# A graph attention kernel: two row sums of head 2 moved around head 1's scores, head 1's W2 casts behind a new wait, two roundings of head 2 moved ahead of its sums

## What is computed

```python
def gat_layer(x, W, a_s, a_d, b, edge_index, concat):
    n = x.shape[0]
    H, C = a_s.shape
    h = (x @ W).reshape(n, H, C)
    src, dst = (edge_index[0], edge_index[1])
    alpha_s = jnp.einsum('nhc,hc->nh', h, a_s)
    alpha_d = jnp.einsum('nhc,hc->nh', h, a_d)
    e = jax.nn.leaky_relu(alpha_s[src] + alpha_d[dst], NEG_SLOPE)
    m = jax.ops.segment_max(e, dst, num_segments=n)
    e = jnp.exp(e - m[dst])
    denom = jax.ops.segment_sum(e, dst, num_segments=n)
    alpha = e / (denom[dst] + EPS)
    msg = h[src] * alpha[:, :, None]
    out = jax.ops.segment_sum(msg, dst, num_segments=n)
    ...
h = gat_layer(x, W1, a_src1, a_dst1, b1, edge_list, concat=True)
h = jax.nn.elu(h)
out = gat_layer(h, W2, a_src2, a_dst2, b2, edge_list, concat=True)
...
x = _layernorm(x + out)
```

## Time and profile before

| | us |
|---|---|
| median of 3 executions | 650.02 |
| lowest, highest | 649.62, 650.75 |
| the profiled execution, its own time | 650.08 |
| its span in the profile | 648.3 |
| PE busy in it | 634.2 |
| DVE busy | 514.4 |
| ACT busy | 333.9 |
| POOL busy | 207.3 |

### The profile page before, as it was taken

How to read it: one execution, slowest core, us unless ns; L and a number is a source line. 1 busy time by engine, 2 the same in 40 slices (tenths; PEclk the granted TensorE clock), 3 DMA queues, 4 the chain that set the end, 5 groups by cost and what they waited for, 6 DMA issues and landing times.

```text
span 648.3 us, 9280 instructions
## 1 busy us (share of the span) xinstructions
PE 634.2 (98%) x3418; PEld 542.3 (84%) x3418; DVE 514.4 (79%) x929; ACT 333.9 (52%) x562; POOL 207.3 (32%) x121
## 2 busy tenths in 40 slices
PE   6999999999989999999999999999999999999996
PEld 4766668989868878988899889988998899887885
DVE  8999997798997977466855776566898588899676
ACT  6799991545614644353444544363445444534282
POOL 0000000131653550257224731465126614551230
PEclk9999999999999999999999999999999999999999
DMA  8422420115142620133203240216025401800002
GB/s 304 169 62 86 143 102 25 49 50 195 37 159 90 203 73 1 50 98 124 73 28 95 79 140 26 68 55 191 5 85 184 122 25 50 288 28 1 1 2 98
DMA packets 22173, 59.36 MB, mean 92 GB/s; under 512 B 2544, under 2 KB 2800, under 8 KB 22128
## 3 DMA queue, kind: packets, MB, share of 16 engines
q1 hardware_dynamic: 22128, 58.76, 27.9%
HBM read 54.03 MB, written 4.72 MB: 91 GB/s over the span
## 4 chain that ended last, share of the span: by engine, by line
PE 86%; DVE 11%; issue 2%; ACT 1%; DMA 0%; SPq 0%; DVEq 0%; ACTq 0%
PE O L1193 23%; PE R L1088 10%; PE R L1094 10%; PE R L1091 10%; PE O L1105 9%; PE R L1160 5%; PE R L1166 5%; PE R L1163 5%; PE R L1110 1%; DVE hl L711 1%; DVE junk L814 1%; DVE junk L686 1%; DVE rb L772 1%; PE O L1160 1%; PE O L1163 1%
## 5 line engine op out<-in xcount | busy, mean ns | idle before, releaser
L1022 POOL TENSOR_TENSOR W2l<-Wr,W2h 128x768 fp32r<-128x768 f32 x48 | 95.3, 1996 | 212.7 <-ACT W2h L405 212.7
L1026 POOL TENSOR_TENSOR Pl<-L,Ph 128x512 fp32r<-128x512 f32 x34 | 54.0, 1598 | 169.2 <-ACT Ph L454 169.2
L1088 PE MATMUL R<-W1h,xTh 128*128 128x384 f32 x312 | 105.8, 339 | 0.0
L1094 PE MATMUL R<-W1h,xTl 128*128 128x384 f32 x312 | 104.8, 336 | 0.0
L1091 PE MATMUL R<-W1l,xTh 128*128 128x384 f32 x312 | 104.8, 336 | 0.0
L686 DVE CUSTOM_DVE_ANT_0 junk<-h,abc 128x768 bf16<-128x768 f32 x64 | 64.4, 1007 | 41.1 <-ACT h L417 36.8
L1193 PE MATMUL O<-W2h,gh 128*128 128x256 f32 (+1 forms) x384 | 78.1, 338 | 0.0
L1193 PE MATMUL O<-W2h,gl 128*128 128x256 f32 (+1 forms) x384 | 77.1, 336 | 0.0
L1193 PE MATMUL O<-W2l,gh 128*128 128x256 f32 (+1 forms) x384 | 77.0, 335 | 0.0
L417 ACT COPY h<-R 128x384 f32<-128x384 f32 x62 | 29.5, 477 | 80.9 <-PE R L1094 72.4
L1160 PE MATMUL R<-Ph,hh 128*128 128x512 f32 x168 | 66.8, 398 | 2.6 <-DVE rb L772 1.7
(11 more groups left out here) (178 smaller groups left out, 1175.4 us busy)
## 6 DMA issues: line engine op xcount, KB each, us to landing
Wr<-in_W SPq DMA_DIRECT2D x101, 384.0 KB, 3.3
abc<-in_as SPq DMA_DIRECT2D x9, 384.0 KB, 4.4
abc<-in_ad SPq DMA_DIRECT2D x9, 384.0 KB, 6.0
h_rows<-h SPq DMA_DIRECT2D x8, 384.0 KB, 2.3
hl<-h_rows SPq DMA_DIRECT2D x8, 384.0 KB, 5.6
xin<-in_xT SPq DMA_DIRECT2D x6, 256.0 KB, 6.5
xr<-in_x SPq DMA_DIRECT2D x1, 1536.0 KB, 7.7
out<-res SPq DMA_DIRECT2D x4, 384.0 KB, 2.3
```

What stands on the lines that cost most here:

```text
L1022: e.tensor_tensor(W2l[:, m % N2, :], Wr[:, n, :], W2h[:, m % N2, :].bitcast(f32), ALU.subtract).then_inc(s_w2l, 1)
L1026: e.tensor_tensor(Pl[:, t, d0:d1], L[:, t, d0:d1], Ph[:, t, d0:d1].bitcast(f32), ALU.subtract).then_inc(s_Pl, 1)
L1088: e.matmul(bank[:, 0:HALF], xTh[:, f, xs], hi[:, ws], start=f == 0, stop=False)
L1094: m = e.matmul(bank[:, 0:HALF], xTl[:, f, xs], hi[:, ws], start=False, stop=f == FT - 1)
```

## The change

Four edits, all in heads 1 and 2, and all in the order of work or in what it waits for; nothing is computed in another way.

```diff
@@ scalar_program, head 1
                     high_w2(0, 4)
                     high_w2(0, 5)
+
+                    e.wait_ge(s_hl, 2 * NT)
                     for k in range(3):
                         high_w2(1, k)
@@ scalar_program, head 2
                     scores(2, 2, 0, NT, ring_bank("r2", 2, 0), ...)
+                    high_h(2, 0)
+                    high_h(2, 1)
                     high_sums(2)
-                    for t in range(NT):
-                        high_h(2, t)
+                    high_h(2, 2)
+                    high_h(2, 3)
                     for k in range(3, FT):
                         high_w1(3, k)
@@ vector_program
-            def sums_P(h):
+            def sums_P(h, between=None):
 
                 e.wait_ge(s_sd, 3 * h + 2)
                 e.scalar_tensor_tensor(
                     out=y2[:, :], in0=y2[:, :], scalar=EPS / 128, in1=rb[:, :], op0=ALU.add, op1=ALU.add).then_inc(s_sd, 1)
+                if between:
+                    between()
                 e.wait_ge(s_dh, h)
@@
                 if h == 1:
-                    scores(1, 1, 0, NT, ring_bank("r1", 1, 0), 6)
-                    sums_P(1)
-                    for t in (2, 3):
+                    def sums_2(t):
                         e.wait_ge(s_h32, 16 + 2 * t + 2)
                         sums_h(2, t, h32[:, t % 2, :], abc[:, 0, :, :])
+                    sums_2(2)
+                    scores(1, 1, 0, NT, ring_bank("r1", 1, 0), 6)
+                    sums_P(1, lambda: sums_2(3))
                     for t in range(NT):
                         low_h(1, t)
                     maxima(2, 0, NT, ring_bank("as", 2, 0))
                 if h == 2:
                     scores(2, 2, 0, NT, ring_bank("r1", 2, 0), 9)
-                    sums_P(2)
-                    for t in range(NT):
+                    sums_P(2, lambda: low_h(2, 0))
+                    for t in range(1, NT):
                         low_h(2, t)
```

## The result

| | before | after |
|---|---|---|
| median, us (six executions each) | 650.12 (649.62 to 650.75) | 653.84 (653.55 to 654.59) |
| the profiled execution, us (its span) | 650.08 (648.3) | 653.91 (652.0) |

The ratio is 1.0058, with a 95% interval of 1.0048 to 1.0068: slower, by 3.7 us. The forecast of 651.6 had the sign, but the time is 2.2 us above it, and 0.3 us above the end of the range at 653.5.

What follows compares the result with a forecast made beforehand. DVE's chain from the scores to the reciprocal in heads 1 and 2 was taken to decide, with PE 98% busy. Head 1's -1.8 and head 2's +3.3 made +1.5 on 650.08: 651.6 us, range 649.8 to 653.5.

Steps and rivals of the forecast that it cites:

- turn by turn list: Head 1, DVE: L872 to 174.8, `hl` 0 to 177.4, `hl` 1 to 179.9, each standing for one W2l of 1.85 us.
- rival 4: Head 2: the long PE stand drops TensorE to 1.2 GHz, a 2.8 us chunk takes 5.6; 654.4 us, 7%.
- the paragraph: Head 2: DVE's reordered low part gains 0; ACT's earlier casts let two W1l go ahead, losing 3.3 us.
- rival 1: Head 1: the four-column operations don't stand one by one, or POOL's third W2l is late; gain 2.6, 650.8 us, 15%.
- rival 2: Head 2: `hl` 2 gets in first, only one W1l goes ahead; +1.65, so 649.9 us, 10%.
- rival 3: Head 2: POOL's W1l makes no one stand; 648.3 us, or 647.5 with the full gain, 11%.
- rival 5: Head 1 gains nothing, as tile 2's sum delays the scores and W2l come worse; head 2 loses; 653.4 us, 5%.
- the sum, -1.8 + 3.3: Head 1's reciprocal comes earlier, gaining 1.8 us; head 2's comes later behind two W1l turns, losing 3.3; +1.5 in all.

Runs made afterwards that it cites:

- Edit 4: In head 2, ACT rounds two rows ahead of the sum, DVE forms one row's low part ahead of the sum's; alone on the kernel before: 654.65 us.

## Why the prediction missed

**Right, with the sizes.** PE no longer stands for the sums of head 2. The stand of DVE ahead of head 1's scores took the sums of tile 2 for nothing. `hl`, zm and mc stood where the turn by turn list puts them, all 0.7 us later on the clock of the span, as C is: zm ends at 186.90 and mc at 188.71, the reciprocal starts at 188.89. Head 1 gained 1.87 for 1.8. POOL won two turns in head 2 and no more, 3.35 for 3.3; PE stood 1.15 and 2.77 where rival 4 says 1.1 and 2.9. Edit 4's DVE half was worth nothing, as the paragraph says. Rivals 1, 2, 3 and 5 are out: mc did stand, two W1l went ahead, they do block, and head 1 gained.

**The Trainium skill's rule** on the shared ports ("SBUF — State Buffer", section "SBUF: two separate sides": an exclusive lock for a whole instruction) is borne out by the traces: an operation on 128x4 elements stood 1.6 us for one W2l, and one on 128x768 stood 1.65 to 1.7. Who asks first is what these edits changed besides the order they speak of.

**Wrong: the sum, -1.8 + 3.3, has no term for TensorE's clock.** The prediction foresaw the stand of 1.1 and 2.9 us, but made the clock's fall behind it a rival with 7% and left it out of the range. It came true together with the forecast. Its evidence was one row at full clock, with a stand of 0.83 us, and a stand of 3.9 was to be judged by it. Nothing in the trace of before bore 3.9 us; that row could not count against the fall. The time of rival 4 should have been an end of the range, and by its mechanism the forecast with the clock's term, not without it, is what occurred, in all five profiled executions with a stand of some 2.5 us or more. "TensorE: Matmul & The Clock Gate", section "Why this matters for your kernels", in the Trainium skill warned of this, and the traces agree in the direction; the shortest stand that did it here is 2.48 us.

**Its price was wrong as well,** on the other side: 2.8 us for a chunk of 2.8 at half speed, where R2 to B grew by 1.35 (1.55 in the other four). The lower clock lasted seven to nine matmuls, each 0.2 us later, and not the twelve of a chunk. In the first trace of the changed kernel its 3.4 us began 0.4 us before PE resumed; in the other four they began 0.1 to 1.1 us after, and cost 0.2 more. With 1.35 the forecast would have been 653.0, and the same range around it would have held 653.84.

**The rest,** 0.75 us ahead of C, is no effect of the edits that I can show. The start of C lies between 161.2 and 163.1 us in the thirteen profiled executions, and in the pair shown here most of the difference arises within the first 11 us, where PE keeps longer to the slow pace with which it begins:

```profile
5.12 5.49 PE L1112 MATMUL O<-ohd,ohs 128*128 128x512 bf16 x12 [5.12 <-DVE ohs L656]
10.05 1.01 PE L1214 MATMUL R<-W1h,xTh 128*128 128x384 f32 x2
```

Before, these twelve took 5.01 us and the next two 0.70. This is TensorE's clock once more. Before, the twelve start 0.43 us apart at first and 0.22 at the end; in the changed kernel they keep to 0.43. The clock record of the trace begins, with the full clock, at 9.43 us before and at 10.70 after. (That the clock of before is full in all 40 slices, as said ahead of the change, leaves this start out: nothing is recorded ahead of 9.43 us.) In the thirteen traces this moment lies between 7.75 and 11.16 us, and C by and large starts later where it is later; the repeat of the same changed kernel has 7.75, where its first trace has 10.70. So the 0.75 us most likely belong to the single execution and not to the edits. What stays open is why the first six executions of the changed kernel lay 0.9 us over what C to B accounts for, and the five of the repeat only 0.1; the mean clocks above suggest longer stretches at the lower clock, and no trace shows them.

## What to carry to other kernels

An engine that shares a port takes turns by who asks first, so a reordering on a third engine (here two casts on ACT, moved ahead of a third) can hand the turns of a critical chain away: list who asks when, within tenths, before moving anything that feeds POOL. Hold back low-priority work until the last link of the critical chain, however small (from C to B, a gate behind `hl` saved 0.15 us, the same gate behind the last four-column operation 1.0). And when a change lengthens a stand of PE to the 2.5 us that were enough here, add the price of the lower clock to the forecast instead of keeping it as an unlikely rival. If the stand can't be avoided, break it with matmuls that are ready; here that spared most executions the fall, not all.

## What the runs showed of the hardware

- One stand of 2.48 us took TensorE from 2.4 to 1.2 GHz, and so did 1.15 and 2.77 us with one matmul between, in all five traces that have them. Stands of 0.83 us did not, nor did 0.68, 1.53 and 1.39 us with matmuls between in the one trace of them; by their mean clocks, four of the eleven executions with these pieces probably had a fall.
- In the traces the fall cost 1.35 to 1.56 us, whether the stand was 2.5 or 3.9 us long, so the shorter stand didn't make it cheaper. The mean clocks of other executions of the same kernels (0.993, where the trace has 0.995) suggest that it can last longer.
- An operation of DVE on 128x4 elements can take 1.79 us for 0.16, if its operands lie in SBUF and POOL has asked first. Four W2l of POOL delayed the reciprocal by the same sum, within 0.12 us, in both places of the chain where they fell.
- The full clock began between 7.75 and 11.16 us in thirteen traces, and the start of stage C of head 0 varied by 1.9 us with it, in kernels that hardly differ up to there. So times of two single traces compare only as distances from one event to another.
